# Joining the setup of a vision-transformer block with its patch embedding, and reordering transfers in its attention

## The reference

```python
# tokenizer: the image and four copies of it, each zero outside a window shifted by 0 or 8 pixels,
# are concatenated along the channels, cut into 14 x 14 patches of 16 x 16, and multiplied
offsets = [(0, 0), (HP, 0), (0, HP), (HP, HP)]
concat = jnp.concatenate([images] + [_crop_shift_pad(images, oh, ow) for oh, ow in offsets], axis=-1)
h = patches(concat) @ W + b                       # 196 tokens of 192 features
h = concatenate([cls_tok, h], axis=1)             # 197 tokens

# attention of 6 heads of 32 on the layer-normed h
q, k, v = (xn @ Wq.T, xn @ Wk.T, xn @ Wv.T)
scores = q k^T * 32**-0.5 + lam * (q . (anchor_w @ anchors))
h = h + (softmax(scores) v) @ Wo.T

# quantised feed-forward on the layer-normed h
x_int8 = clip(round(layernorm(h) / 0.02), -128, 127)
h = h + (x_int8 @ weight_t) * 0.0002 + bias
```

## Time and profile before

| what | value |
|---|---|
| median of three runs | 1951.77 us |
| profiled execution, its own time | 1955.63 us |
| its span, first to last instruction | 1954.0 us |
| mean granted clock of TensorE | 0.98 |
| busy: PE, DVE, ACT, POOL | 93%, 75%, 42%, 38% of the span |
| setup block | 0 to 44 us |
| token block | 44 to 470 us |
| attention block | 470 to 1954 us |

### The profile page before, as it was taken

The page is one execution under the profiler, slowest core; times in us unless marked ns, Lnnn a source line. Parts: engine busy times, 40 slices in busy tenths (PEclk is TensorE's granted clock), DMA queues, the critical chain, the costliest instruction groups (busy, mean ns, idle before and its releaser), DMA issues.

```text
span 1954.0 us, 55344 instructions
## 1 busy us (share of the span) xinstructions
PE 1810.5 (93%) x16960; PEld 1660.4 (85%) x16960; DVE 1460.4 (75%) x3716; ACT 813.0 (42%) x1941; POOL 734.7 (38%) x1891
## 2 busy tenths in 40 slices
PE   1999999996799999999999999999999999999996
PEld 1989889885799888888888888888888888888885
DVE  6778778776577777777777777777777777777773
ACT  2000000000455555555555555555555555555552
POOL 4234434433043433334334343333433333333343
PEclk9999999998899999999999999999999999999995
DMA  8999999993455555555555555555555555555540
GB/s 199 206 290 252 280 289 248 290 283 135 122 132 129 131 132 121 134 126 129 134 121 135 125 128 136 121 136 123 128 135 121 133 128 125 137 122 131 129 117 22
DMA packets 210926, 303.41 MB, mean 155 GB/s; under 512 B 47680, under 2 KB 199923, under 8 KB 200004
## 3 DMA queue, kind: packets, MB, share of 16 engines
q1 hardware_dynamic: 206900, 266.59, 57.4%
q0 software_dynamic: 3984, 36.28, 4.8%
HBM read 126.49 MB, written 58.29 MB: 95 GB/s over the span
## 4 chain that ended last, share of the span: by engine, by line
PE 40%; SPq 17%; DMA 12%; issue 5%; ACT 1%; POOL 1%; DVE 1%; ACTq 0%; POOLq 0%; DVEq 0%
DMA k_st<-k_lo 11%; SPq L636 9%; PE o_bank L772 8%; PE bank L712 7%; PE bank L744 5%; PE bank L756 5%; PE bank L721 3%; PE bank L695 3%; PE o_bank L782 2%; SPq L674 2%; PE o_bank L695 2%; PE bank L732 1%; PE bank L733 1%; PE bank L734 1%; PE bank L818 1%
## 5 line engine op out<-in xcount | busy, mean ns | idle before, releaser
L970 DVE TENSOR_REDUCE neg_max<-bank 99x2 f32<-99x394 f32 x768 | 419.7, 560 | 207.5 <-PE bank L744 207.1
L901 ACT ACTIVATE probs<-bank 99x396 f32<-99x396 f32 x768 | 386.1, 503 | 331.1 <-PE bank L756 331.0
L430 PE MATMUL bank<-e_t,xt 128*128 128x192 f32 x2352 | 405.5, 334 | 46.2 <-DVE xt L447 46.2
L430 PEld LDWEIGHTS bank<-e_t,xt 128*128 128x128 f32 x2352 | 383.4, 192 | 68.3 <-DVE xt L447 58.0
L744 PE MATMUL bank<-k_st,q_st 96*99 96x198 f32 x1536 | 272.2, 272 | 43.8 <-DMA k_st<-k_lo 40.3
L756 PE MATMUL bank<-q_st,k_st 98*99 98x198 f32 x1536 | 289.1, 270 | 3.2 <-ACT probs L901 3.1
L772 PE MATMUL o_bank<-probs,vals 99*64 99x198 f32 (+1 forms) x3072 | 290.3, 337 | 0.2
L772 PEld LDWEIGHTS o_bank<-probs,vals 99*64 99x64 f32 (+1 forms) x3072 | 210.8, 137 | 50.3 <-issue 0.9
L895 ACT ACTIVATE x_hi<-bank 128x396 fp32r<-128x396 f32 x128 | 63.4, 495 | 451.3 <-PE bank L695 451.3
L744 PEld LDWEIGHTS bank<-k_st,q_st 96*99 96x99 f32 x1536 | 188.2, 166 | 70.4 <-issue 58.5
L1080 POOL TENSOR_TENSOR hb<-h,ffn_bias 99x384 f32<-99x384 f32 x128 | 128.7, 1006 | 294.5 <-DVE h L1013 294.5
(11 more groups left out here) (124 smaller groups left out, 3979.0 us busy)
## 6 DMA issues: line engine op xcount, KB each, us to landing
x_t<-in_x_dram SPq DMA_DIRECT2D x56, 1344.0 KB, 20.1
q_st<-q_hi SPq DMA_DIRECT2D x256, 148.5 KB, 3.9
k_st<-k_hi SPq DMA_DIRECT2D x256, 148.5 KB, 3.7
xn_in<-xn_scratch SPq DMA_DIRECT2D x128, 148.5 KB
q_st<-q_lo SPq DMA_DIRECT2D x128, 148.5 KB, 3.8
k_st<-k_lo SPq DMA_DIRECT2D x128, 148.5 KB, 3.8
h_in<-h_scratch SPq DMA_DIRECT2D x128, 148.5 KB
h_scratch<-h_t POOLq DMA_DIRECT2D x13, 1344.0 KB, 14.3
```

Of the source, the lines that this page charges most:

```text
L430: last = pe.matmul(token_bank(p)[:, 0:D], xt[:, p, c // 3, c % 3, :], e_t[:, row_kind(t), col, c // 3, c % 3, :], start=c == 0, stop=c == 5)
L901: nc.scalar.activation(probs[:, n.slot, h, :, :], wide(T_BANK, TC), ACT.Exp).then_inc(exp_done, 1)
L970: nc.vector.tensor_reduce(out=neg_max[:, n.slot, :, h], in_=wide(S_BANK[h % 2], TC)[:, :, 0:NTOK], axis=AX_X, op=ALU.max, negate=True).the ...
```

## The change

- The setup and the token blocks become one. The host passes the attention weights already turned and stacked by halves, and the token weights in the order 1, 3, 0, 2, 4 of their five groups, in five transfers with semaphores of their own. The first pixel row comes in two halves of its columns. PE no longer turns weights.
- Pixel rows: SP issues the transfers to partitions 0 to 63, ACT those to 64 to 127.
- The anchors' work is done ahead of the crops, on DVE; the low parts of the attention weights are made by DVE in row 1; the BOTTOM crops by POOL during row 0; TOP's right kinds by DVE between the first two transposes.
- In the token loop DVE turns token j+1 before it adds up j-1.
- The first token's sum waits for both biases (`biases_landed` at 32), the second of which is SP's last transfer ahead of row 1.
- POOL stores h of a row ahead of its norm. Of the last row it norms and stores the first 8 tokens (`EARLY`) in the token block; the attention block norms and stores the other 6.
- In the attention, SP's order is: stackings of d, out[k], load_xn(ahead), h_in[b], maxima of a. PE turns f's tokens ahead of `score(a, 4)`.

The core of the diff:

```diff
@@ token block, sync
+            for g, landed in ((1, left_landed), (2, left_landed), (3, right_landed), (4, right_landed), (0, whole_landed)):
+                load(w_of[g], s["tok_w"][:, RAW_ORDER.index(g)], landed)
+            load_half_row(sp, 0, (0, 1), x_half[0])
+            load(tok_bias[:], ..., biases_landed)
+            load_half_row(sp, 1, (0, 1), x_half[1])
+            for i, w in enumerate(("wq", "wk", "wv")):
+                load(w_raw[:, i, :, :], s[w], small_landed)
+            load(wo_raw[:], s["wo"], small_landed)
+            load(ffn_raw[:].bitcast(mybir.dt.int32), ..., small_landed)
+            load(ffn_bias[:], ..., biases_landed)
             def step(t):
-                for q in range(4):
-                    sp.dma_start(x_t[32 * q:32 * q + 32, t.slot, :, :], x_rows[t.n, q]).then_inc(x_landed[t.slot], 16)
+                load_row(sp, t, (0, 1))
@@ token block, scalar
+            act.wait_ge(left_landed, 32)
+            load_half_row(act, 0, (2, 3), x_half[0])
+            load_half_row(act, 1, (2, 3), x_half[1])
...
+            def step(t):
+                if t.reuses(2):
+                    act.wait_ge(turned, t.count(G, -G))
+                    load_row(act, t, (2, 3))
@@ token block, vector
             def step(t):
-                dve.wait_ge(x_landed[t.slot], t.landed(64))
                 for j in range(G):
-                    turn(t, j)
+                    if opens(t, j):
+                        dve.wait_ge(x_half[0], 256)
+                        turn(t, 0)
+                        add(right[:, :, 1:3, :], w_of[0][upper, :, 1:3, :], w_of[3][upper, :, 1:3, :])
+                        turn(t, 1)
+                        dve.wait_ge(crops_made, 11)
+                        masked_add(right, w_of[1][upper], m_right, upper)
+                        continue
+                    if j + 1 < G:
+                        turn(t, j + 1)
+                    elif not (t.fixed and t.n == G - 1):
+                        dve.wait_ge(x_landed[t.plus(1).slot], row_landed(t.plus(1)))
+                        turn(t.plus(1), 0)
+                    if t.fixed and t.n == 0:
+                        if j == 1:
+                            dve.wait_ge(crops_made, 12)
+                            dve.wait_ge(biases_landed, 32)
...
+                    if t.fixed and t.n == 1:
+                        if j == 2:
+                            dve.wait_ge(w_high, 8)
+                            low_weights(Q)
...
@@ token block, gpsimd
+                if not last:
+                    pool.dma_start(h_dram[:, bass.ds(at_token, G), :], h_t[:, p, 0:G, :]).then_inc(h_stored[p], 16)
                 st = stats[:, p, 0:T, :]
@@ attention block, sync
-                if ahead.within(B):
-                    load_xn(ahead)
-                if b.within(B):
-                    ... h_in[b]
                 if d.within(B):
                     ... six stackings
-                if a.within(B):
-                    ... maxima of a
                 if k.within(B):
                     ... out[k]
+                if ahead.within(B):
+                    load_xn(ahead)
+                if b.within(B):
+                    ... h_in[b]
+                if a.within(B):
+                    ... maxima of a
@@ attention block, tensor
                     turn_back(c)
-                if has_a:
-                    score(a, 4)
                 if has_f:
                     ...
                     turn(MISC[2], xn_in, f, DA).then_inc(xt_done, 1)
+                if has_a:
+                    score(a, 4)
@@ attention block, vector
-            for j in range(G):
+            for j in range(EARLY, G):
                 nc.vector.tensor_scalar(xn_t[:, j, :], h_t[:, LAST, j, :], ...).then_inc(last_row_xn, 1)
```

More of the change, by code:

```diff
@@ L381, in build_tokens, with crop, by_group, grouped @@
     xn_stored = sem("xn_stored")
+    SMALL = 16 * 5
+    ROW = "p g (r w) -> p g r w"
+    HALF = IMG * CH // 2
+    def crop(row, col, p=slice(0, 128)):
+        return e_t[p, row, col]
+    def by_group(ap):
+        return ap.rearrange("p (j g d) -> p g d j", g=2, d=HD)
+    def grouped(ap):
+        return ap.rearrange("p (g d j) -> p g d j", g=2, d=HD)
     def token_bank(p):
         return banks[4 + p]
+    def load_row(eng, t, quarters):
+        for q in quarters:
+            eng.dma_start(x_t[32 * q:32 * q + 32, t.slot, :, :], x_rows[t.n, q]).then_inc(x_landed[t.slot], 16)
+    def load_half_row(eng, half, quarters, landed):
+        cols = slice(half * HALF, half * HALF + HALF)
+        for q in quarters:
+            dst = x_t[32 * q:32 * q + 32, 0, :, :].rearrange(ROW, r=QR)[:, :, :, cols]
+            src = x_rows[0, q].rearrange(ROW, r=QR)[:, :, :, cols]
+            for g in range(4):
+                eng.dma_start(dst[:, g], src[:, g]).then_inc(landed, 16)
+    def row_landed(t):
+        return t.before(64) if t.slot == 0 else t.landed(64)
     def rows(eng, step):
@@ L436, in _, with add, masked_add @@
         @block.vector
         def _(dve):
-            nc.vector.memset(h_t[:, 1, G, :], 0.0).then_inc(zeros_made, 1)
+            def add(out, a, b):
+                nc.vector.tensor_tensor(out, a, b, ALU.add).then_inc(crops_made, 1)
+            def masked_add(out, pair, mask, p):
+                nc.vector.scalar_tensor_tensor(out=out[:, :, 1, :], in0=pair[:, :, 1, :], scalar=mask[p, 0:1],
+                                               in1=out[:, :, 1, :], op0=ALU.mult, op1=ALU.add).then_inc(crops_made, 1)
@@ new lines, in low, with low_weights @@
+            def low(dst, src, hi, i):
+                if i == K:
+                    ins = nc.vector.scalar_tensor_tensor(out=dst, in0=src, scalar=SCALE, in1=hi.bitcast(F32),
+                                                         op0=ALU.mult, op1=ALU.subtract)
+                else:
+                    ins = nc.vector.tensor_tensor(dst, src, hi.bitcast(F32), ALU.subtract)
+                ins.then_inc(prep, 1)
+            def low_weights(i):
+                low(wa_lo[:, i, :], w_raw[:, i, 0, :], wa_hi[:, i, :], i)
+                low(wb[DB:2 * DB, i, :], w_raw[DB:2 * DB, i, 1, :], wb[DB:2 * DB, i, :], i)
@@ new lines, in _ @@
+            full, left, right = (crop(MID, col) for col in (INTERIOR, LEFT, RIGHT))
+            dve.wait_ge(left_landed, 32)
+            add(left_pair, w_of[1], w_of[2])
+            dve.wait_ge(right_landed, 32)
+            add(right_pair, w_of[3], w_of[4])
+            dve.wait_ge(whole_landed, 16)
+            dve.wait_ge(crops_made, 2)
+            add(left, w_of[0], left_pair)
+            dve.wait_ge(crops_made, 3)
+            add(full, left, right_pair)
+            dve.wait_ge(masks_made, 2)
@@ new lines, in _ @@
+            dve.wait_ge(crops_made, 4)
+            masked_add(left, right_pair, m_left, everything)
+            add(right[:, :, 1:3, :], w_of[0][:, :, 1:3, :], right_pair[:, :, 1:3, :])
+            dve.wait_ge(crops_made, 6)
+            masked_add(right, left_pair, m_right, everything)
+            full, left, right = (crop(TOP, col, upper) for col in (INTERIOR, LEFT, RIGHT))
+            add(left, w_of[0][upper], w_of[1][upper])
+            dve.wait_ge(crops_made, 8)
+            add(full, left, w_of[3][upper])
```

389 lines of the change are left out of this document (184 added, 205 removed).

## The result

| | before | after |
|---|---|---|
| median | 1952.57 us (1950.19 to 1955.41, 4 runs) | 1877.63 us (1875.92 to 1879.13, 4 runs) |
| ratio, 95% interval | 1 | 0.9615 (0.9599 to 0.9632) |
| profiled execution, its span | 1955.6, 1954.0 us | 1878.2, 1876.3 us |

What follows compares the result with a forecast made beforehand. PE was busy 1810.5 of 1954.0 us, so only its waits or slow stretches could give time back. Start and token loop 53, last row 5 and attention 37 make 95 us: forecast 1858 us, range 1842 to 1894.

Steps and rivals of the forecast that it cites:

- step 1: Setup joined to embedding: first matmul at 25 us, 21 saved; added wait for both biases until 31, PE stops about 3.
- step 4: Pixel loads on two queues: 387 to 425 GB/s if side by side, and the 17.3 us of waits go.
- step 5: Last row at the change of stage: shorter norm, store and POOL chain save 5 us, range 1 to 7.
- rival E: Setup: x halves and late bias put the first token's sum at 42 us, not 31; 1869 us; chance within the forecast's 0.67.
- Steps 2 and 3: Token loop: turning ahead removes 0.19 us waits, 18 us; work moved beside rows costs 2.5 us of PE, crops 2.
- the margin of 0.1 us: Token loop: DVE's sum is ready about 1.8 us after release, PE needs it at 1.935; without margin, 0 to 20 us lost.
- Rival B: Pixel loads: the two queues take turns, rows come late, 10 to 48 us, typically 25; 1883 us; chance 0.16.
- if POOL is late, up to 3: Last row: if POOL is late with its eight tokens, up to 3 us is lost.
- Step 6: Attention: SP issues stackings first, so waits for k_lo go; 0.34 us per image, 37 us taken, 41 at most.
- Rival C: Attention: k_lo's landing takes over 4.8 us, every image waits again and 37 us are gone; 1895 us; chance 0.13.
- Rival D: Attention: next tokens' loads come too late, about 2008 us at 1.2 us over the critical delay; chance 0.02.
- Step 7: Attention: tokens' transposes ahead of score 4, taken as 0 us, bounds -3 to +6.

Runs made afterwards that it cites:

- e2: Kernel after, bias still last, but ACT issues its half of pixel row 1 only when the small weights have landed: 1866.21 us.
- e1: Kernel after with ffn_bias loaded right behind tok_bias instead of last: 1868.49 us.
- e6: Kernel after with DVE's token loop in the order of before (turn j, then sum and statistics of j-1): 1897.69 us.
- e5: Kernel after with all four quarters of pixel rows 2 to 13 on SP's queue: 1906.37 us.
- e11: Kernel after, pixel rows 1 to 13 still on two queues, but both write the same half of the partitions at a time: 1908.41 us.
- e4: Kernel after with SP, not POOL, storing the first 8 normed tokens of the last row: 1875.37 us.
- e3: Kernel before with SP's new order in the attention and nothing else: 1921.27 us.
- e8: Kernel before with PE's new order alone, next tokens turned ahead of score 4: 1950.29 us.
- e9: Kernel after with ffn_bias early, attention weights behind SP's part of row 1, and the last row's early store on SP: 1859.98 us.
- e10: e9 with ACT's part of row 1 issued only when the second half of row 0 has landed: 1865.95 us.

## Why the prediction held, and where its 20 us went

Direction and stages were right, and so were the mechanisms, but for the bytes ahead of the bias (step 1), the rate of the pixels (step 4) and the end of the block (step 5). Between the profiled spans 77.7 us were gained, 17.3 less than 95; the medians differ by 74.9, as the profiled execution before lay 3.1 us above its median. Taken apart by the prediction's own steps, 15.3 + 3.3 + 1.5 - 3.0 make 17.1 of them:

- **Step 1, the added wait (the mis-sized term).** Predicted: both biases landed at 31 us, PE stops for about 3. Measured: 46.3 and 18.3 us, 15.3 too little. The sum counted 6.7 MB on SP's queue and 2.75 beside it on ACT's. It left out ACT's half of row 1, 2.75 MB more, issued at 20.31 us: by 46.3 us ACT's queue had moved 5.51 MB. And it counted bytes as if both queues moved them alike, where small packets in turn with large ones get far less than their half. With 2.76 MB on ACT's queue, as the sum has it, the first sum is made at 31.6 us and PE waits 4.4 (e2); 31 and 3 were predicted. An estimate of the two parts: at 20.3 us SP had 2.0 MB left ahead of the bias; had the queues shared by bytes, 4 MB in all would have been enough, and they had moved by about 35 us. So some 4 us are the bytes left out and some 12 the turns by packet. The prediction had the late bias as rival E with the sum at 42 us; that was nearer, and still 4 short. In the difference of medians the bias is worth 9.1 (e1) to 11.4 us (e2), since after it the pixels become the limit.
- **Step 1, first matmul.** 22.0 us instead of 25: 3.0 better, near the range's lower end (21).
- **Steps 2 and 3, the loop.** From the first matmul to the last sum, without the 18.3 us, it took 388.2 us; the prediction's terms were 379 + 3 + 2.5 + 2 + 1.5 = 388. That the sums agree is in part luck, for the single terms don't. The 2 us for POOL's crops beside the token sums are nothing: in e1 five sums beside them (27.5 to 36.2 us) took 0.32 us each, and in the kernel after most of the crops ran while PE stood still. The first two tokens took 6.55 us, where two take 3.90 in the loop, at a granted clock of 1.00; why is open. The other terms were not tested one by one; the clock's part is seen at 46 to 54 us. Turning ahead was put at 18 and is 20.1 (e6), and the margin of 0.1 us was there: no idle moment of PE in 300 us.
- **Step 4, pixels.** The waits of 17.3 us went, as said, but not for the reason given: two queues make 257 GB/s, far from 387 to 425. At 257 a row of 5.5 MB takes 21.4 us and 27.9 are covered, so it suffices, and that the time came out was luck as far as the rate goes; with the stores the loop moves 303 GB/s at a share of 0.93. Rival B's rate (206 to 218) is what e5 and e11 have, and there it costs 28.7 us in e5, near the 25 that B was given. Two queues on two halves are between the two theories, closer to B in rate and wholly with the forecast in time.
- **Step 5, last row.** 1.7 instead of 5. Measured by parts: the factors 1.4 shorter (5.07 to 3.68 us from POOL's first instruction to DVE's norm), the norm 2.3, the store 1.8, together 5.5, where 5.3 were added up and 5 taken. What was left out is that POOL's store, issued 0.3 us before the last sum, holds up the block end for 3.9 us more (4.61 against 0.67); e4 gets 2.9 of them back. The prediction's "if POOL is late, up to 3" had the right place and not the reason: POOL's norm was in time, its transfer was not.
- **Step 6, SP's order.** 35.5 of 37, by e3 this order's alone. Rival C (a late k_lo) did not come: with stores and loads behind it, k_lo lands faster, 2.6 us instead of 3.8. Rival D has no sign in the waits.
- **Step 7, PE's order.** Put at 0; e8 gives 0 to 6 us for it in the kernel before, too small to split further.

What stays open: the last 1 us of the block end, and how the 4 us of e9's pixel wait can be had without e10's later one.

## What to carry to other kernels

A wait that a change adds is priced by when its data land, and that is not bytes over bandwidth: count what every queue has issued by then and look at its packet sizes, and load the little that many wait for first (9 us for one line moved). When POOL's last act in a block is a transfer of its own, the next block begins only behind it (4.6 us here); the same store on SP cost 1.7. Where a stage was limited by one queue that fills partitions by halves, a second queue on the other half is worth a test, even if it gives a quarter and not the double.

## What the hardware showed that was not expected

- 192 KB of weights in rows of 1536 bytes took 24.9 us from issue to landing beside a queue of 10,752-byte pieces, and 11.5 us when those came later (after, e2), on an unchanged queue. From 30 to 40 us the two queues moved 196 and 194 packets, and 1.92 and 0.26 MB.
- Pixels alone: 208 GB/s on one queue, 216 on two queues in the same half of the partitions, 230 to 240 on one queue alternating halves, 257 on two queues in different halves. The DMA share is 1.00 to 1.04 in the windows shown, so a share of 1 does not say that the rate can't rise.
- A block end after a store issued by POOL: 4.6 us from the last statistics to the next block's first instruction; with the same store on SP 1.7 us.
- The SBUF-to-SBUF stackings land in 2.6 to 2.7 us instead of 3.7 to 3.8 when the image loads are issued behind them, not ahead of them, though the bytes are the same.
